# Fetching one tile in 64 with single-row transfers issued by SyncE, in a graph layer whose other gathers GpSimd issues

## What is computed

```
h        = relu(layernorm(x))
messages = concat(h[src], edge_attr) @ W_message      # 256 + 64 features in, 256 out
agg      = segment_sum(messages, dst)
a        = layer_norm(relu(agg) + h) * scale + bias
out      = x + layer_norm(h + mlp(a)) * scale + bias  # mlp: three layers of 256, with skips
```

## Time and profile before

| | |
|---|---|
| median of three runs | 2260.93 us |
| profiled execution | 2263.02 us, of which the span of the trace is 2261.2 us |
| TensorE busy (matmul) | 74% of the span |
| GpSimd busy | 71% |
| VectorE, ScalarE busy | 42%, 16% |
| DMA | 357.81 MB, mean 158 GB/s |
| mean granted TensorE clock | 0.937 of full speed |

### The profile page before, as it was taken

One profiled execution on the slowest core, in us unless ns is written; L12 is line 12 of the kernel. 1 busy time (PEld: TensorE's weight loads), 2 busy tenths in 40 slices (PEclk: granted clock), 3 DMA queues, 4 the chain that ended last, 5 costly groups with the idle time before them and its releaser, 6 DMA issues.

```text
span 2261.2 us, 35804 instructions
## 1 busy us (share of the span) xinstructions
PE 1672.8 (74%) x6729; PEld 1128.5 (50%) x6730; DVE 957.0 (42%) x3949; ACT 364.2 (16%) x1114; POOL 1594.7 (71%) x1687
## 2 busy tenths in 40 slices
PE   0058778878878777788778778778787887777876
PEld 0035545545555545555555555555554555555544
DVE  8444334434434434443433433443443434434434
ACT  2601111111111111111111111111111111111112
POOL 0067777777777777777777777777777777777770
PEclk9999999999999999999999999998998999999997
DMA  6775555555555555555555555555555555555542
GB/s 234 276 189 158 156 155 155 150 159 155 155 158 154 156 159 150 161 157 149 159 155 155 156 150 161 157 160 149 159 157 151 161 149 158 161 147 161 154 123 61
DMA packets 361302, 357.81 MB, mean 158 GB/s; under 512 B 250208, under 2 KB 303776, under 8 KB 361120
## 3 DMA queue, kind: packets, MB, share of 16 engines
q0 software_dynamic: 81888, 231.06, 34.7%
q1 hardware_dynamic: 218768, 69.94, 12.4%
q10 hardware_dynamic: 60464, 55.28, 7.3%
HBM read 329.65 MB, written 26.48 MB: 157 GB/s over the span
## 4 chain that ended last, share of the span: by engine, by line
POOL 62%; issue 21%; PE 8%; DMA 3%; DVE 1%; POOLq 0%; ACT 0%; DVEq 0%; ACTq 0%
POOL ring L281 62%; PE acc_banks L361 4%; DMA ring<-h_table,src_all 2%; PE agg_bank L313 1%; PE agg_bank L319 1%; PE y_bank L295 1%; PE z_bank L295 1%; PE acc_banks L369 0%; POOLq L277 0%; PE z_bank L305 0%; ACT xs L437 0%; DMA h_table<-xs 0%; PE st_bank L330 0%; POOLq L279 0%; ACT r_bank L411 0%
## 5 line engine op out<-in xcount | busy, mean ns | idle before, releaser
L281 POOL DMA_INDIRECT ring<-h_table,src_all x1664 | 1586.0, 953 | 527.2 <-issue 519.6
L361 PE MATMUL acc_banks<-ring,onehot 128*128 128x320 f32 x3328 | 1112.2, 483 | 518.8 <-issue 310.0
L361 PEld LDWEIGHTS acc_banks<-ring,onehot 128*128 128x128 f32 x3328 | 659.9, 209 | 933.5 <-issue 773.7
L670 DVE TENSOR_SCALAR onehot<-iota,dst_rel 128x128 f32<-128x128 f32 x1664 | 360.6, 303 | 249.2 <-issue 200.7
L480 DVE TENSOR_TENSOR w<-agg_bank,h_late 128x256 f32<-128x256 f32 x103 | 43.7, 424 | 953.8 <-PE agg_bank L319 953.8
L399 ACT ACTIVATE uT<-z_bank,fp 128x128 f32<-128x128 f32 x200 | 80.6, 453 | 1482.0 <-PE z_bank L305 1482.0
L313 PE MATMUL agg_bank<-wm,ST 128*128 128x256 f32 (+1 forms) x594 | 166.4, 401 | 0.0
L313 PEld LDWEIGHTS agg_bank<-wm,ST 128*128 128x128 f32 (+1 forms) x594 | 106.5, 192 | 54.9 <-issue 34.6
L319 PE MATMUL agg_bank<-wl,u 128*128 128x256 f32 x408 | 118.5, 414 | 6.3 <-DVE z L518 6.3
L295 PEld LDWEIGHTS y_bank<-u,wl 128*128 128x128 f32 x808 | 108.8, 196 | 5.6
L295 PE MATMUL y_bank<-u,wl 128*128 128x128 f32 x808 | 109.0, 279 | 0.0
(11 more groups left out here) (109 smaller groups left out, 919.1 us busy)
## 6 DMA issues: line engine op xcount, KB each, us to landing
ring<-edges SPq DMA_DIRECT2D x208, 256.0 KB, 3.7
ring<-h_table,src_all POOLq DMA_INDIRECT x1664, 2.8
h_late<-h_table ACTq DMA_DIRECT2D x103, 128.0 KB
x_late<-x ACTq DMA_DIRECT2D x103, 128.0 KB
h_in<-h_table ACTq DMA_DIRECT2D x100, 128.0 KB
xs<-x POOLq DMA_DIRECT2D x14, 896.0 KB, 6.5
h_table<-xs SPq DMA_DIRECT2D x14, 896.0 KB, 4.2
out<-o ACTq DMA_DIRECT2D x98, 128.0 KB
```

The costliest lines, as they stand in the source:

```text
L281: nc.gpsimd.indirect_dma_start(out=ring[:, k * G + j, 0:D], out_offset=None, in_=h_table, in_offset=bass.IndirectOffsetOnAxis(ap=src_all[: ...
L361: return nc.tensor.matmul(acc_of(at), onehot[:, (k % OG) * G + j, :], ring[:, k * G + j, :], start=False, stop=True, skip_group_check=True)
L670: op = nc.vector.tensor_scalar(onehot[:, (k % OG) * G + j, :], iota[:, :], dst_rel[:, bass.ds(g * G + j, 1)], None, ALU.is_equal)
```

## The change

The last tile of each round (slot 63) is no longer gathered by GpSimd: it issues 63 gathers a round. SP fetches the 128 rows of that tile, each by a DMA of its own (1 KB from `h_table` to one lane of the slot), with the row number in a register.

- After its last store to `h_table`, SP waits until all these stores have landed, and then loads the indices of the 26 tiles to partition 0 of SBUF (over the buffer `xs`, whose use has ended), with 26 DMAs of 128 numbers each. It waits for them before it issues the first edge attributes.
- In each round, behind the eight issues of edge attributes, SP loads four times 32 registers and issues 32 row DMAs after each load.
- TensorE waits, for slot 62, for one gather instead of two, and for slot 63 for the four semaphores `rows_in`, 32 DMAs each.

```diff
+BY_ROW = 32
...
+        rows_flat = xs[0:1, :, :, :].rearrange("p s b d -> p (s b d)")[:, 0:ROUNDS * P].bitcast(I32)
+        row_src = rows_flat.rearrange("a (i p) -> a i p", p=P)
...
+            for s in range(XS):
+                sp.wait_ge(h_stored[s], 16 * len(range(s, NX, XS)))
+            for i in range(ROUNDS):
+                sp.dma_start(row_src[:, i, :], src[0:1, :, i * RT + RT - 1], allow_slow_non_contiguous=True).then_inc(row_src_in, 16)
+            sp.wait_ge(row_src_in, 16 * ROUNDS)
+            row_regs = registers(nc.sync, BY_ROW)
             with nc.sync.Fori(0, passes) as p:
                 with nc.sync.Fori(0, ROUNDS) as i:
                     for k in range(RG):
                         sp.wait_ge(group_free, p * NG + i * RG + k + 1)
                         sp.dma_start(ring[:, k * G:(k + 1) * G, D:F],
                                      edges[0, :, bass.ds((i * RG + k) * G, G), :]
                                      ).then_inc(edges_in[k], 16)
+
+                    for c in range(P // BY_ROW):
+                        at = numbers(nc.sync, row_regs, rows_flat, i * P + c * BY_ROW, NB * P - 1)
+                        for q in range(BY_ROW):
+                            lane_at = c * BY_ROW + q
+                            sp.dma_start(ring[lane_at:lane_at + 1, RT - 1, 0:D], h_table[bass.ds(at[q], 1), :]
+                                         ).then_inc(rows_in[c], 16)
...
-                    for j in range(G):
+                    for j in range(G if k < RG - 1 else G - 1):
                         nc.gpsimd.indirect_dma_start(
...
+                        def rows_of(j):
+                            slot = k * G + j
+                            if slot >= RT - PT:
+
+                                if slot == RT - PT:
+                                    pe.wait_ge(gathered[slot // PT], (p * ROUNDS + i + 1) * (16 * (PT - 1)))
+                                else:
+                                    for c in range(P // BY_ROW):
+                                        pe.wait_ge(rows_in[c], (p * ROUNDS + i + 1) * (16 * BY_ROW))
+                            elif j % PT == 0:
+                                pe.wait_ge(gathered[slot // PT], (p * ROUNDS + i + 1) * (16 * PT))
...
                         for j in range(G - 1):
+                            rows_of(j)
                             tile(j)
-                        if (G - 1) % PT == 0:
-                            pe.wait_ge(gathered[k * PAIRS + (G - 1) // PT], (p * ROUNDS + i + 1) * (16 * PT))
+                        rows_of(G - 1)
                         with nc.tensor.If(closes > 0):
                             pe_visit(pe, visit, nc.s_assert_within(steered[VSEL], 0, 1), close)
                         tile(G - 1).then_inc(group_free, 1)
```

More of the change, by code:

```diff
@@ L187, in build @@
         gathered = [sem(f"gathered{q}") for q in range(RG * PAIRS)]
+        row_src_in = sem("row_src_in")
+        rows_in = [sem(f"rows_in{c}") for c in range(P // BY_ROW)]
         edges_in = [sem(f"edges_in{k}") for k in range(RG)]
@@ L355, in _ @@
                         pe.wait_ge(onehots, p * NG + g + 2)
+                        def rows_of(j):
[8 more added lines that the diff above has]
+                                pe.wait_ge(gathered[slot // PT], (p * ROUNDS + i + 1) * (16 * PT))
                         def tile(j):
-                            if j % PT == 0:
-                                pe.wait_ge(gathered[k * PAIRS + j // PT], (p * ROUNDS + i + 1) * (16 * PT))
                             at = nc.s_assert_within(steered[j], 0, 1)
```

## The result

The changed kernel takes 2231.14 us in the median of four runs (2229.23 to 2232.03), the kernel before 2260.49 beside it: a ratio of 0.987 (95% interval 0.985 to 0.989). It is 1.3% faster. I had predicted 2489 us, 10% slower. The time is that of the first rival, GpSimd as the bound, at 2228 us.

The account below looks back on a forecast made before the run. GpSimd's issue bounds the kernel before; SP was to become the bound at 67.8 + 11.6 + 9.0 + 0.3 = 88.7 us a round. Start 134.8, 26 rounds, landing 2.8 and end 45.3 gave 2489 us (range 2226 to 2700).

Parts of the forecast that it names:

- the first rival: Main loop: GpSimd stays the bound, SP's round under 79.2 us, row DMAs at 0.456 us or less; 2228 us, chance 0.21.
- (a): SP's 128 row DMAs a round: 0.53 us each from start to start, 67.8 us a round.
- my low end: SP's row DMAs: 0.38 us each, 0.33 for the DMA and 0.05 of gap, no register work; 48.6 us.
- What GpSimd sheds: GpSimd's gathers: 26 fewer at 1.258 us, 32.7 us in all; its round falls from 80.5 to 79.2 us.
- (b) Register loads: SP's four loads of 32 registers a round: 2.9 us each with bounding and address, 11.6 us a round.
- the rival of single loads: SP's register loads go one by one: 21.6 us a round more, 110.3 in all, 3051 us; chance 0.08.
- (c) Edge DMAs: SP's eight edge-attribute DMAs a round, issued together behind the rows: 9.0 us, between 5.5 and 10.5.
- (d) The loop: Branch and address work of SP's loop: 0.3 us a round.
- Ahead of the loop: SP's setup: 12 us issuing 26 index DMAs, 5 us for pieces and landing; first round starts at about 134.8 us.
- On TensorE: TensorE's five register-value waits a round for one: under 0.5 us; extra DMA load 136 us on each engine, 6%.
- The sum: Whole kernel: SP's start at 134.8, 26 rounds of 88.7, 2.8 for landing, 45.3 for the end; 2489 us.
- The break-even: SP's row DMA at 0.456 us, where SP's round would equal GpSimd's 79.2 us.

Follow-up runs that it names:

- loads_one_by_one: The changed kernel with the table of row numbers starting 4 bytes later, nothing else; 2679.2 us, ratio 1.184 to the kernel before.
- edges_first: The changed kernel with round 0's edge attributes issued before the index DMAs, the loop then rows(i), edges(i + 1) over 25 rounds; 2299.5 us, ratio 1.015.
- index_loads_alone: The kernel before with only SP's wait for the table and the 26 index DMAs, GpSimd gathering all 64 tiles; 2265.1 us, ratio 1.000.

## Why the prediction was wrong

The step that failed is (a), the 128 row DMAs, put at 0.53 us each and 67.8 a round. They start 0.41 us apart in the median, 52.5 a round: 15 us less. I took the issue price of the nearest rows, all of them DMAs over 128 lanes, and wrote that the size helps nothing. The size doesn't, but the shape does: one row in one piece is the cheapest of the forms tried, 0.225 us with a register address, and the rows I leaned on were all of another shape. Even my low end, 0.33 for the DMA itself, was too high. I had put a bound under a value with rows that could not bound it, since none had few rows to move; only the low end of the whole row, 0.38, reached past the measured 0.41, since it left out the register work. The rival of GpSimd as the bound had the time right and the way there wrong: it wanted the addresses of 32 rows worked out together and the DMA at its 0.373. In the trace 3224 of the 3328 rows have a FUSED_REGOPS of their own, and the DMA takes 0.225.

The other steps, by their terms:

- **What GpSimd sheds**: 32.7 us expected; its gathers end 32.1 us sooner. Right.
- **(b) Register loads**: nearly right in size, 2.04 us against 2.3, and the start at a multiple of 16 bytes is what they hang on; the rival of single loads was wrong here, and its price, 0.21 us a register, is shown by `loads_one_by_one`.
- **(c) Edge DMAs**: 9.0 us expected, 11 measured, 1.08 us each in the median. Where SP was the bound they took 0.71 (`loads_one_by_one`).
- **(d) The loop**: 0.3 us expected, 2.7 measured on average. In the kernel before the jump takes 0.2 us; with 128 row DMAs and their register operations in the body it takes more than ten times that. In another layout, 4.9. This term, put at almost nothing, makes 2.2 of the 2.9 us a round by which `edges_first` is slower than the changed kernel.
- **Ahead of the loop**: SP's first round starts at 139.6, not 134.8 (an index DMA of 128 single numbers holds SP for 0.6 us). With SP's rows left out it costs nothing: `index_loads_alone`. With them it uses up what SP gains on GpSimd in the loop.
- **On TensorE**: its new waits are hidden. The DMA load of the rows, which entered no sum, was put 16 times too high: 2 packets a row, not 32.
- **The sum**: the rule by which a round of SP over 79.2 us sets the time is right to 0.2% in six runs, with the 46.6 us of the end as the rest. The mechanism of the forecast is real: a longer round of SP does set the time. By the same rule the changed kernel comes out at 139.6 + 26 x 78.6 + 46.6 = 2230 us, against a span of 2227.4: SP and GpSimd end level, and with SP's late start the threshold is nearer 78.5 us than 79.2. The Trainium skill's 512 cycles, "DMA: Bandwidth & Descriptors", § Why a DMA increments its semaphore by 16 and not by 1, which the prediction turned into an estimate of 0.43 us, don't agree with this trace: a row DMA took 0.225.

The break-even that I gave, 0.456 us a row, was the most useful number of the text: the measured 0.41 is under it by 6 us a round, of which the edge DMAs (about 2) and the jump (2.4) took most. What I should have weighed is that none of my rows showed a DMA of one lane. A chance of 0.21 for the other side of a threshold that the forecast round passed by only 12% (88.7 against 79.2 us) was too low. That the round came out under it by so little is luck in part: with the jump of `edges_first` it would have been over.

What stays open: why a row cut into pieces costs 0.51 to 0.56 us, more than 128 rows of 1 KB at 0.43; why a cut row costs more still among whole rows; why two lanes of 127 numbers cost more than two of 128; and what sets the stall at the jump. That SP costs the changed kernel anything at all (0.985 against 0.987) isn't shown: the intervals overlap.

## What to carry to other kernels

When a change gives a queue many small transfers, price the issue from a transfer of the same shape. If the trace has none, say that the bound is missing instead of taking the nearest row. When one engine's issue is the bound and another sequencer is to take a share, compare their work by round, the jump of the loop and a late start included: below the bound it costs nothing, above it every microsecond counts once a round. And read from the trace that an edit is really in the program (packets, number of instructions) before its time is believed.

## What the runs showed of the hardware

- A DMA issue holds SP for 0.25 us with one row, 0.32 with 16, 0.58 with 128 rows of 256 bytes, with constant addresses. One row cut in two or sixteen pieces: 0.53 to 0.60. With a register address: 0.225 for a whole row, 0.507 for sixteen pieces, 0.562 for two, and 0.61 to 0.68 for two where whole rows stand between.
- SP loads 32 registers in 2.04 us from a table that starts with its buffer, and in 6.66 us from 4 bytes beyond. TensorE loads 12 in 0.855 us from every fourth of its entries of 52 bytes, and in 2.87 us from the others.
- The jump back in SP's loop takes 0.2 us with a short body, and on average 2.7 and 4.9 us with a long one in two layouts.
- In the median the edge DMAs landed 6.2 us after their issue, 3.7 before, and the gathers 4.5 in place of 2.8; neither reached the bound.
- One chip ran the kernel before in 3379 us, half as long again, and two rounds written out in a loop in 3771, where elsewhere they are 1.5% faster than the kernel before.
